# Half of the key, stack and value fills of an attention batch inside its neighbour's loop, copied by VectorE

## The reference

```python
x = x + jnp.tanh(g_ffn[0]) * _L0_ffn_ref(_layernorm(x), router_w, gate_w, up_w, down_w)
x = x + jnp.tanh(g_xattn[1]) * _L1_xattn_ref(_layernorm(x), ctx_2048, ctx_2048, mask, w_q, w_k, w_v, w_o, b_o)
# _L1_xattn_ref: 32 query heads of 8 channels, 8 key and value groups, 4 heads to a group
q = (Q @ w_q.T).reshape(B, S, G, HG, HD)
k = (K @ w_k.T).reshape(B, S, G, HD)
v = (V @ w_v.T).reshape(B, S, G, HD)
scores = jnp.einsum('bnghd,bmgd->bnghm', q, k) / scale      # then key padding and causal mask
attn = jax.nn.softmax(scores, axis=-1)
out = jnp.einsum('bnghm,bmgd->bnghd', attn, v).reshape(B, S, D)
return out @ w_o.T + b_o
```

## Time and profile before

| | |
|---|---|
| median of 3 executions | 400.14 us (399.49 to 401.64) |
| profiled execution | 402.57 us |
| its span in the profile | 399.6 us |
| TensorE busy, share of the span | 343.4 us, 86% |
| VectorE, ScalarE, GpSimd busy | 210.5, 164.7, 100.9 us |
| mean granted TensorE clock | 0.932 of full |

### The profile page before, as it was taken

One profiled execution on the slowest core, in us unless ns is written; L12 is line 12 of the kernel. 1 busy time (PEld: TensorE's weight loads), 2 busy tenths in 40 slices (PEclk: granted clock), 3 DMA queues, 4 the chain that ended last, 5 costly groups with the idle time before them and its releaser, 6 DMA issues.

```text
span 399.6 us, 4567 instructions
## 1 busy us (share of the span) xinstructions
PE 343.4 (86%) x1470; PEld 207.2 (52%) x1477; DVE 210.5 (53%) x501; ACT 164.7 (41%) x344; POOL 100.9 (25%) x156
## 2 busy tenths in 40 slices
PE   2999886529999847999799989988879989999997
PEld 1485675316665534555463655453343535444886
DVE  5143874502222267799436935792141339778921
ACT  2433443213333122246872875396785223333000
POOL 7102663520000377102340434045243001000000
PEclk9999997558999656999999999999999999999999
DMA  6995000152111127100000000000000000000011
GB/s 213 383 419 138 1 15 2 65 175 75 54 40 54 46 77 282 57 6 0 8 1 2 0 7 2 1 0 8 0 1 2 0 2 0 0 0 3 25 41 39
DMA packets 13880, 22.41 MB, mean 56 GB/s; under 512 B 2033, under 2 KB 11249, under 8 KB 13042
## 3 DMA queue, kind: packets, MB, share of 16 engines
q1 hardware_dynamic: 13090, 20.03, 14.5%
q0 software_dynamic: 768, 2.10, 1.6%
HBM read 15.83 MB, written 6.03 MB: 55 GB/s over the span
## 4 chain that ended last, share of the span: by engine, by line
PE 60%; DVE 16%; ACT 9%; issue 6%; POOL 4%; DMA 3%; another core or an unknown queue 0%; SPq 0%; ACTq 0%; DVEq 0%; POOLq 0%
PE bank L230 45%; DVE mx L1169 8%; ACT region L895 5%; PE bank L442 5%; PE bank L410 3%; POOL x_sorted L709 2%; PE bank L413 2%; DVE stats L966 2%; PE bank L243 1%; DVE x_sb L1006 1%; POOL rstd L682 1%; PE bank L237 1%; ACT qst L846 1%; DMA x_sb<-in_x_dram 1%; PE bank L490 1%
## 5 line engine op out<-in xcount | busy, mean ns | idle before, releaser
L1169 DVE TENSOR_REDUCE mx<-bank 128x2 f32<-128x512 f32 (+1 forms) x96 | 60.2, 684 | 13.9 <-PE bank L413 8.3
L895 ACT ACTIVATE region<-bank,padcol 128x512 f32<-128x512 f32 x96 | 60.7, 701 | 12.0 <-PE bank L230 11.0
L745 POOL TENSOR_SCALAR_AFFINE_SELECT region<-region 128x1024 f32<-128x1024 f32 x32 | 35.0, 1094 | 94.4 <-ACT region L895 94.0
L230 PE MATMUL bank<-xT,e_gu 128*128 128x512 f32 x128 | 57.6, 594 | 0.5 <-ACT xT L762 0.5
L230 PE MATMUL bank<-qst,kblk 128*128 128x512 f32 x96 | 46.0, 506 | 2.3 <-ACT amat L904 0.8
L410 PE MATMUL bank<-kblk,qst 128*128 128x512 f32 x96 | 44.3, 488 | 2.6 <-ACT qst L846 1.5
L230 PEld LDWEIGHTS bank<-xT,e_gu 128*128 128x128 f32 x128 | 23.4, 191 | 25.0 <-issue 24.2
L413 PE MATMUL bank<-causb,identb 128*128 128x256 bf16 (+1 forms) x89 | 28.9, 324 | 0.0
L678 POOL TENSOR_SCALAR veps<-mv 128x1 f32<-128x1 f32 x40 | 11.4, 286 | 67.3 <-DVE mv L968 65.1
L230 PE MATMUL bank<-e_down,region 128*128 128x256 f32 x128 | 27.8, 380 | 0.0
L1006 DVE SCALAR_TENSOR_TENSOR x_sb<-bank,tg,x_sb 128x256 f32<-128x256 f32 x24 | 11.6, 483 | 30.7 <-PE bank L230 30.6
(11 more groups left out here) (156 smaller groups left out, 551.9 us busy)
## 6 DMA issues: line engine op xcount, KB each, us to landing
e_gu<-in_e_gu_dram SPq DMA_DIRECT2D x2, 1408.0 KB, 12.6
x_sorted<-zero SPq DMA_DIRECT2D x1, 1920.0 KB, 10.2
y_sorted<-region SPq DMA_DIRECT2D x15, 128.0 KB, 1.7
x_sb<-in_x_dram SPq DMA_DIRECT2D x4, 256.0 KB, 4.0
ctxT<-in_ctxT_dram SPq DMA_DIRECT2D x2, 512.0 KB, 7.4
e_down<-in_e_down_dram SPq DMA_DIRECT2D x1, 1024.0 KB, 13.7
region<-x_sorted SPq DMA_DIRECT2D x1, 1024.0 KB, 7.4
e_gu<-in_f_gate_dram SPq DMA_DIRECT2D x1, 1024.0 KB, 4.9
```

The lines of the kernel that those rows point to most:

```text
L230: return pe.matmul(dst, lhsT, rhs, start=first, stop=last)
L745: pool.affine_select(out=block, in_=block, compare_op=ALU.is_ge, fill=0.0, base=0, pattern=[[0, 2], [0, PER_GROUP], [1, P]], channel_multi ...
L895: taken(act.activation(dst, src.rearrange("p (h n) -> p h n", n=SEQ - mt * P), ACT.Exp, bias=padcol[:, key:key + 1], scale=float(HD) ** -0 ...
L1169: taken(dve.reduce_max(mx[:, b % 2, nt, quads, q, hg], src, AX), "sa")
```

## The change

1. Routing reads the logits and the rank row in PSUM; the copies `logit` and `r_s[6]` go. The last two tiles of the first layer norm are written by VectorE (`xn1_last`) instead of ScalarE, without GpSimd's `shift` step.
2. `projections(b)` is split off `keys(b)`. All four stand where `keys(0)` stood; `khl` has a place for each batch.
3. `FIRST_LEAD` = 7: only seven scores of batch 1 stand ahead of batch 0's weights; the loop of batch 0 carries 17 scores instead of 12, and its `neg_turn` stands at n = 18 instead of 15.
4. For batches 2 and 3, ks0 is filled at n = 13 of the loop two batches before, and the stack pieces 0 and 1 at n = 19 and 21; all three use "max" banks and are copied by VectorE. ks1 and pieces 2 and 3 stay behind the loop, with ScalarE as copier (ks1 was VectorE's); ScalarE now copies the pieces before the keys.
5. Value fills of half 0 stand at n = 20 and 22 of the batch's own loop, on "max" banks, copied by VectorE. The two of half 1 stay behind the loop, with six scores behind each.

```diff
@@ -29,10 +29,13 @@
 FFN_MT = FFN_I // P
 FFN_BLOCKS = FFN_I // 4 // P
 LEAD = 12
+FIRST_LEAD = 7
 QUERIES_AT = 10
 
 NORM_STEPS, LATE_NORM_STEPS = (13, 15, 17, 19), (3, 4, 6, 7)
-NEGATE_AT = 15
+KEYS_AT, STACK_AT = 13, (19, 21)
+VALUES_AT = (20, 22)
+NEGATE_AT, FIRST_NEGATE_AT = 15, 18
 LN_EPS, GN_EPS = 1e-5, 1e-3
 MASKED = -float(2.0 ** 100)
 DEAD = -3.0e38
...
@@ -212,6 +214,14 @@
             q, c = divmod(n, 12)
             return (q, c // 2, 0, slice(c % 2 * 2, c % 2 * 2 + 2)) if c < 8 else (q, c - 8, 1, slice(0, 4))
 
+        def stack_fill(b, piece):
+
+            if b < 2:
+                return "qs", 4 * b + piece
+            return ("qd", 2 * (b - 2) + piece) if piece < 2 else ("qs", 8 + 2 * (b - 2) + piece - 2)
+
+        VALUE_STAGES = ("av0", "av1")
+
         def tile_cols(k):
             return slice(k * P, (k + 1) * P)
 
...
-                pe.wait_ge(sem(f"xn{layer}"), k + 1)
+                if layer == 1 and k >= TILES - 2:
+                    pe.wait_ge(sem("xn1_last"), k - TILES + 3)
+                else:
+                    pe.wait_ge(sem(f"xn{layer}"), k + 1)
...
@@ -387,13 +396,17 @@
                         w = GROUPS * HD
                         ins = mm(dst[:, r * w:(r + 1) * w], ctxT[:, t, tile_cols(2 * b + r)], wv[:, t, :], t == 0, t == KT - 1)
                 ready(ins, "vp")
+
+            def keys(b, one, halves=range(HALVES)):
+
+                seq = slice(b * SEQ, (b + 1) * SEQ)
                 if b == 0:
                     pe.wait_ge(sem("sel_made"), 2)
                     pe.wait_ge(sem("padrow_made"), 1)
                 pe.wait_ge(sem("kp_taken"), b + 1)
-                for q in range(HALVES):
+                for q in halves:
                     dst = acquire(pe, f"ks{q}", b, one)
-                    mm(dst[:, 0:SEQ], selr[:, (8 + q) * P:(9 + q) * P], khl[:, s, :], True, False)
+                    mm(dst[:, 0:SEQ], selr[:, (8 + q) * P:(9 + q) * P], khl[:, b, :], True, False)
                     ready(mm(dst[:, 0:SEQ], padselr[:, :], padrow[:, seq], False, True), f"ks{q}")
 
             def scores(b, n):
@@ -402,7 +415,8 @@
                 q, hg, nt, quads = score_fill(n)
                 if n % 12 == 0:
                     pe.wait_ge(sem(f"ks{q}_taken"), b + 1)
-                    pe.wait_ge(sem("qs_taken"), 4 * b + 2 + 2 * q)
+                    stage, i = stack_fill(b, 2 * q + 1)
+                    pe.wait_ge(sem(stage + "_taken"), i + 1)
                 if n == 0:
                     if b == 0:
                         loaded(pe, "caus", 2)
...
 
 
+            projections(0, "main")
             keys(0, "main")
+            for b in range(1, BATCH):
+                projections(b, "main")
 
             def slot_turn(i):
                 if i in SORTED_LOADS:
@@ -525,30 +544,38 @@
                 queries(1, n)
                 if n >= 20:
                     stack_piece(1, n - 20, "exp")
-            for n in range(LEAD):
+            for n in range(FIRST_LEAD):
                 scores(1, n)
                 if n == 2:
                     neg_turn(0, ("turn1", "tok1"))
             for b in range(BATCH):
+                lead = LEAD if b else FIRST_LEAD
                 for n in range(24):
-                    if b + 1 < BATCH and n + LEAD < 24:
-                        scores(b + 1, n + LEAD)
+                    if b + 1 < BATCH and n + lead < 24:
+                        scores(b + 1, n + lead)
                     weights(b, n)
                     if b >= 1 and n % 2 == 1:
                         finish(b - 1, n // 2)
                     if b + 2 < BATCH:
                         queries(b + 2, n)
+                        if n == KEYS_AT:
+                            keys(b + 2, "max", (0,))
+                        if n in STACK_AT:
+                            stack_piece(b + 2, STACK_AT.index(n), "max")
                     if b == BATCH - 1 and n in NORM_STEPS:
                         ln_turn(3, NORM_STEPS.index(n), "tok1")
-                    if n == NEGATE_AT and b + 1 < BATCH:
+                    if n in VALUES_AT:
+                        values(b, VALUES_AT.index(n), "max")
+                    if n == (NEGATE_AT if b else FIRST_NEGATE_AT) and b + 1 < BATCH:
                         neg_turn(b + 1, ("turn1", "turn1"))
                 if b + 2 < BATCH:
-                    keys(b + 2, "wide")
-                    query_stack(b + 2, "wide")
-
-                for i in range(4):
-                    values(b, i)
-                    for n in range(i * LEAD // 4, (i + 1) * LEAD // 4):
+                    keys(b + 2, "wide", (1,))
+                    for piece in (2, 3):
+                        stack_piece(b + 2, piece, "wide")
+
+                for i in range(2):
+                    values(b, 2 + i, "wide")
+                    for n in range(i * LEAD // 2, (i + 1) * LEAD // 2):
                         if b + 2 < BATCH:
                             scores(b + 2, n)
 
...
                     inverse_std(1, k - 3, LN_EPS)
+                if 3 <= k < TILES + 1:
                     pool.wait_ge(sem("rstd1"), k - 2)
                     pool.tensor_scalar(shift[:, k - 3:k - 2], mv[:, 1, k - 3, 0:1], rstd[:, 1, k - 3:k - 2], -1.0,
...
                     if b == BATCH - 1 and n in NORM_STEPS:
                         ln_turn(3, NORM_STEPS.index(n))
-                    if n == NEGATE_AT and b + 1 < BATCH:
+                    if n == (NEGATE_AT if b else FIRST_NEGATE_AT) and b + 1 < BATCH:
                         neg_turn(b + 1)
                 if b + 2 < BATCH:
+                    query_stack(b + 2)
                     keys(b + 2)
-                    query_stack(b + 2)
                 value_turn(b)
 
             def magnitude(i):
...
 
+            for k in (TILES - 2, TILES - 1):
+                tile = HALF_ORDER[k]
+                dve.wait_ge(sem("rstd1"), k + 1)
+                dve.tensor_scalar(xn1[:, tile, :], x_sb[:, tile, :], mv[:, 1, k, 0:1], rstd[:, 1, k:k + 1],
+                                  ALU.subtract, ALU.mult).then_inc(sem("xn1_last"), 1)
+
             steps = [0]
 
...
+            step(dve.reduce_max(r_s[:, 0, :], src, AX))
+            step(dve.tensor_tensor(out=r_a[:, :, :], in0=src, in1=each(r_s[:, 0, :], EXPERTS), op=ALU.is_equal))
 
             step(dve.tensor_tensor(out=r_b[:, :, :], in0=r_a[:, :, :], in1=each(small_c[:, 8:16], TILES, 1), op=ALU.mult))
             step(dve.reduce_max(r_s[:, 1, :], r_b[:, :, :], AX))
             dve.tensor_tensor(out=onehot16[:, :, :], in0=r_b[:, :, :], in1=each(r_s[:, 1, :], EXPERTS), op=ALU.is_equal)\
...
                 if b < 2:
                     dve.wait_ge(sem("blocks_clear"), HALVES * (b + 1))
-                src = filled(dve, "ks1", b)
+                q = 1 if b < 2 else 0
+                src = filled(dve, f"ks{q}", b)
                 for j in range(QUADS):
                     rows = slice(32 * j, 32 * j + 32)
-                    ins = dve.tensor_scalar(kblk[s][1][rows, j, :], src[rows, 0:SEQ], small_c[rows, 1:2], None, ALU.add)
-                taken(ins, "ks1")
+                    ins = dve.tensor_scalar(kblk[s][q][rows, j, :], src[rows, 0:SEQ], small_c[rows, 1:2], None, ALU.add)
+                taken(ins, f"ks{q}")
+
+            def stack_copy(b, piece):
+
+                stage, i = stack_fill(b, piece)
+                src = filled(dve, stage, i).rearrange("p (h n) -> p h n", h=2)
+                dve.wait_ge(sem("sb_ready"), 24 * (b - 2) + 12)
+                taken(dve.tensor_scalar(qst[:, b % 2, 0, 2 * piece:2 * piece + 2, :], src, small_c[:, 0:1], None, ALU.add),
+                      stage)
 
             key_low(0)
             spread_keys(0)
+            for b in range(1, BATCH):
+                key_low(b)
 
             def slot_product(i):
                 src = filled(dve, "sg", i)[:, EXPERT_I:2 * EXPERT_I]
@@ -1181,6 +1227,13 @@
                     dve.scalar_tensor_tensor(out=nmx[:, s, nt, HEADS:2 * HEADS], in0=m, scalar=-1.0,
                                              in1=nmx[:, s, nt, 0:HEADS].bitcast(F32), op0=ALU.mult,
                                              op1=ALU.subtract).then_inc(sem("nm_made"), 1)
+
+            def value_copy(b, nt):
+
+                src = filled(dve, "av0", 2 * b + nt)
+                if b >= 1:
+                    dve.wait_ge(sem("avT_ready"), 8 * (b - 1) + 4 * nt + 4)
+                taken(dve.tensor_copy(avT[nt][:, 0, :], src), "av0")
 
             def finish(b, n):
...
             negate(0)
             for b in range(BATCH):
+                lead = LEAD if b else FIRST_LEAD
                 if b + 1 < BATCH:
-                    for n in range(LEAD):
+                    for n in range(lead):
                         row_maxima(b + 1, n)
                 for n in range(24):
-                    if b + 1 < BATCH and n + LEAD < 24:
-                        row_maxima(b + 1, n + LEAD)
-                        if n + LEAD == 23:
```

(12 more changed lines are left out.)

79 lines of the change are left out of this document (37 added, 42 removed).

## The result

The changed kernel takes 397.6 us, the median of 20 executions (395.91 to 400.44), against 400.45 for the kernel before on the same chip (398.81 to 401.64, 20 executions): ratio 0.9929, 95% interval 0.9916 to 0.9942. It is 2.85 us faster; 10.55 had been forecast. The profiled execution took 398.06 us, its span is 395.5.

A forecast was written before the change was run, and what follows sets the result against it. Loops were taken as mostly ScalarE-bound, joints as TensorE-bound. Terms 0.2 + 0.7 + 5.3 + 2.5 + 1.2 + 0.65 = 10.55 us took the median from 400.14 to 389.6 us; range 385.5 to 394.5.

The forecast's parts named there:

- Part 1: Routing: dropped copies save 0.35 us, but the last norm waits out GpSimd's first clear; +0.2 us, bounds -0.4 to +0.9.
- Part 2: Gap behind routing: projections of batches 1 to 3 there raise TensorE's clock for the first slots; +0.7 us, bounds -0.7 to +1.6.
- Part 3: Before loop 0: with five scores less ahead, batch 0's first weights start 2.8 us earlier.
- Parts 4 and 5: Loop 0 grows by 3.5 us, eating the lead's 2.8; after joint 0 the next exponential comes 5.3 us earlier.
- Part 6: Loop 1 and joint 1: last exponential of the loop 2.3 us later, next exponential after the joint 255.4; gain 2.5 us.
- the forecast's own signs of being wrong: Joint scores waiting longer than 1.5 us for ScalarE's copies, or loops 0 and 1 above 24 us.
- Part 7: Loops 2 and 3, only two value fills entering each: gain 1.2 us for loop 2 with joint 2, 0.65 for loop 3.
- VectorE's copies: VectorE's 512-column copy from PSUM, priced without a row at 0.67 us, between 0.48 and twice that.
- The rival with VectorE's banks: In the loops, 14 fills on "max" banks hold TensorE until VectorE frees them: slower, 404.5 us, chance 0.05.
- offset of 2.4 us: Whole execution: the profiled run of the kernel before lay 2.4 us above its median; the forecast median was 389.6.
- loops give back more: Rival: loops 0 and 1 grow by 6 us each, handshakes not being at their best; 394.1 us, chance 0.20.
- nothing measurable: Rival: joints are bound by their 12 maxima and what a joint loses its loop gains; 399 to 401 us, chance 0.04.

The follow-up runs named there:

- e4: The changed kernel with 12 scores of batch 1 again ahead of batch 0's weights (`FIRST_LEAD` back to 12): 399.01 us, ratio 0.9965 to the kernel before.
- e6: The changed kernel with joints reordered: next scores first, remaining fills between them on exponentials' banks, ScalarE copying keys before stack: 391.72 us, ratio 0.9766 to the kernel before.
- e12: The changed kernel with GpSimd's clears behind VectorE's last normalization and each loop's second value fill one step later: 390.91 us, run again 394.07 us.

## Why the prediction was wrong, step by step

From mark to end the forecast terms make 10.55 us, the trace shows 4.3: -0.5 for routing, +0.3 up to slot 0, +2.6 from there to the first exponential, +1.2 in loop 0 and joint 0, +1.0 in loop 1 and joint 1, -0.6 in loop 2 and joint 2, +0.1 in the rest. Three steps failed: the price of the shared port for the last norm, the clock at the first slot, and the walks through loops and joints, which took each handshake at its best. The walks make 5 of the 6.2 us that are missing, 1.0 of it by the clock in loop 2. By terms:

- **Part 1, routing: forecast +0.2, measured -0.5.** The mechanism was right and was named: VectorE's norm waits out GpSimd's clear. Its size failed: the step "by that the new norm waits out the first clear", where the row shows 1.90 us, both clears. The Trainium skill ("SBUF — State Buffer", Who interferes with whom) gives the lock for one instruction; the trace agrees that the norm is held. What happens between two clears that stand back to back, the traces show to be open: the norm was never let in there (1.90 us in seven of seven), the instruction of the earlier trace rows in ten of 17. The forecast took the one outcome that it had seen. The -0.5 itself is the difference of two traces, in a quantity that varies by 0.7.
- **Part 2, projections in the gap: forecast +0.7 in the slots, measured next to nothing** (slot 0 at 30.37 and 30.07, before 30.24; behind the first indirect DMA 0.3 earlier in the trace). "If the clock rises under this work, the slots start at the higher one" was the failing step. The clock rose near 82.5 us and fell right behind TensorE's 3 us pause, as the first gate product began. The reading of the slices behind it was too simple as well: in the earlier trace rows the clock is at 5 tenths where TensorE is at 2 to 5, and at 6 tenths in a slice with 8. Part 1 had made the first indirect DMA 2.2 us later than a free norm does (9.71 against 7.54), so the two misses may be tied together: with the clears behind the norm the clock held in three of seven traces, and slot 0 came 3 us earlier there.
- **Part 3, the lead: right.** Forecast 2.8; slot 0 to the first exponential went from 89.9 to 87.2 us, and e4 gives 2.5 for the lead alone.
- **Parts 4 and 5, loop 0 and joint 0: 1.3 us too good.** Loop 0 grew by 4.0 (forecast 3.5), joint 0 fell by 5.2 (forecast 6.0). The walk of the loop was nearly right: fill 23 at 202.10, 20.7 behind the first exponential, forecast 20.5. The walk of the joint failed, "exponential at t+12.5": it came at t+13.55. Its head was nearly right: the second score, which has to wait for ScalarE's key copies, started at t+4.75 (forecast 4.55). The scores behind it were slower than the walk: the second value fill of the joint was ready for ScalarE's copy at t+9.4 (forecast 8.55), and the six scores behind that took the rest.
- **Part 6, loop 1 and joint 1: forecast 2.5, measured 1.0.** The loop grew by 2.9 instead of 2.3, and the joint fell by 4.0 instead of 4.8. One of the forecast's own signs of being wrong came here, a score that waits longer than 1.5 us for ScalarE's copies:

```profile
244.62 0.50 PE L424 MATMUL bank<-kblk,qst 128*128 128x512 f32 x1 [1.60 <-ACT prod L936]
```

  The walk had put this wait in (score 1 at 6.25 us behind fill 23, measured 6.4), so it isn't what was missed; the scores behind it were slower again, and the exponential came at 15.2 instead of 14.2. It is a wait that the forecast took as given and that e6's order takes out.
- **Part 7: forecast 1.2 and 0.65, measured -0.6 and +0.1.** Loop 2 grew by 2.7. Of that 1.0 goes with the clock that fell to its lower level for some 3 us (e6, where it stayed up, has the loop 1.0 shorter), the other 1.7 with ScalarE's waits of 0.74 and 1.21 behind the value fills, where 0.8 had been put. Joint 2 fell by 2.1.
- **VectorE's copies**, the one price without a row, took 0.75 (stack) and 0.69 us (values) against 0.67 assumed. The rival with VectorE's banks did not come: no wait of TensorE in the attention is put down to one of these copies.
- **From the profile to the median:** the gain of the traces, 4.5 in the executions' times, shrinks to 2.85 in the medians, since the profiled execution of the kernel before lay 2.1 above its median and that of the kernel after only 0.5. The forecast carried its offset of 2.4 us unchanged to the other kernel, as if it were a constant; it belonged to that one execution and is luck. At least part of it is the clock's course: executions of this kernel with a mean granted clock of 0.927 or 0.932 took 400.4 to 402.6 us, those with 0.935 or 0.936 398.8 to 401.1.

No rival named the result: 397.6 lies between "loops give back more" (394.1) and "nothing measurable" (399 to 401). The first had the direction and the reason, handshakes at their best, but not the numbers: loops 0 and 1 together grew by 6.9 us, not 12; most stretches missed by a little, and all in one direction. What was not forecast in any case is that the joints' own order kept 5 us (e6).

## What to carry to other kernels

Work moved into a stretch that another engine paces is free only as far as the mover has idle time there, and it does harm where the pacing engine is served behind it: sixteen products ahead of the last weights made ScalarE wait 1.2 to 1.6 us a loop, of which moving them one step gave back about 1 us in all; the keys and stack pieces in the same loops cost some 1 us. When a part is prepared earlier, reorder its consumer too; here that was worth more than the whole change. And add up a walk of many handshakes with a surcharge: each stretch here came out 0.5 to 1 us worse than its best case.

## What the runs showed of the hardware

- A VectorE tensor_scalar of 0.38 to 0.41 us that starts beside two back-to-back GpSimd clears (1.84 us together) takes 1.90 us; it did so in all seven traces of kernels in which the clears do not wait for it. Another one of the same width, begun 0.25 us into two such clears, took 0.84 us in ten traces (the second clear then took 1.10 us instead of 0.95) and 1.73 in seven, both with the same instructions.
- TensorE's clock went from 1.2 to 2.4 GHz under the projections in the gap and fell again around a pause: after TensorE was busy 1.03 of 4 us it was granted 0.66, after 2.67 of 4 it stayed at 1.00 in one execution, and in others with the same instructions it fell. In loop 2 it fell after 0.44 of 2 us busy. Slot 0 of one program (e12) thus lay at 27.1 in one trace and at 28.9 in another, 0.7 of it from ahead of the first indirect DMA. In e6 it fell although TensorE's longest pause there was 1.50 us.
- The time of an execution lies 1.7 to 3.9 us above its span; comparing spans alone can mislead by more than the effect.
